# Opening a graph-network tile with three slots bank by bank, kept products between the banks

## The reference

```python
h = jnp.maximum(_layernorm(x), 0.0)
weight = jnp.einsum('rb,bio->rio', w_comp, bases)       # 32 relations from 8 bases
h_rel = jnp.einsum('ni,rio->rno', h, weight)
x = x + jax.ops.segment_sum(h_rel[etype, src] * norm, dst, num_segments=n) + h_bias
h = jnp.maximum(_layernorm(x), 0.0)
# second layer: every edge and every self loop, norm = dis[row] * dis[col], dis = rsqrt(degree)
x = x + jax.nn.relu(jax.ops.segment_sum(norm * (h @ W.T + b)[row], col, num_segments=n))
```

## Time and profile before

| | us |
|---|---|
| median of 3 runs | 644.56 |
| lowest, highest | 641.9, 646.03 |
| the profiled execution | 644.92 |
| its span, first to last instruction | 643.0 |
| PE busy in it | 514.1 (80%) |
| POOL busy in it | 342.6 (53%) |

### The profile page before, as it was taken

One profiled execution on the slowest core, in us unless ns is written; L12 is line 12 of the kernel. 1 busy time (PEld: TensorE's weight loads), 2 busy tenths in 40 slices (PEclk: granted clock), 3 DMA queues, 4 the chain that ended last, 5 costly groups with the idle time before them and its releaser, 6 DMA issues.

```text
span 643.0 us, 16581 instructions
## 1 busy us (share of the span) xinstructions
PE 514.1 (80%) x6328; PEld 328.7 (51%) x6328; DVE 320.2 (50%) x894; ACT 151.5 (24%) x272; POOL 342.6 (53%) x466
## 2 busy tenths in 40 slices
PE   2221626658989999989999999998997877889997
PEld 1111515536656666656666556665655555545443
DVE  8995038865465345665654654554643221454121
ACT  3436235432122011221220310302201000240121
POOL 3105707864665776675756747767677777400000
PEclk9555657679999999999999999999999987789999
DMA  9639985654676787785875858868768788523042
GB/s 283 231 125 338 390 299 139 190 144 128 192 224 179 223 264 202 207 260 157 248 225 165 267 155 231 265 194 263 240 195 266 238 239 237 155 55 111 1 97 66
DMA packets 43606, 130.01 MB, mean 202 GB/s; under 512 B 8911, under 2 KB 9536, under 8 KB 43462
## 3 DMA queue, kind: packets, MB, share of 16 engines
q0 software_dynamic: 27040, 99.60, 52.4%
q1 hardware_dynamic: 15004, 27.08, 13.0%
q10 hardware_dynamic: 1482, 2.18, 1.0%
HBM read 120.39 MB, written 11.00 MB: 204 GB/s over the span
## 4 chain that ended last, share of the span: by engine, by line
PE 53%; DMA 9%; DVE 7%; issue 5%; ACT 3%; POOL 2%; ACTq 0%; DVEq 0%
PE PS L1482 23%; PE PS L1462 17%; DMA gath<-rows_layer,srcs 9%; PE PS L1558 7%; PE PS L1502 4%; DVE room_b L1177 2%; POOL gath L672 2%; DVE zt L1177 1%; PE PS L1468 1%; PE PS L1356 1%; ACT room_b L780 1%; PE PS L1491 1%; ACT zt L780 1%; PE PS L1364 1%; DVE sel L1099 0%
## 5 line engine op out<-in xcount | busy, mean ns | idle before, releaser
L672 POOL DMA_INDIRECT gath<-rows_layer,srcs x335 | 334.4, 998 | 198.9 <-PE PS L1468 104.3
L1462 PE MATMUL PS<-sel,gath 128*128 128x48 f16 (+7 forms) x4020 | 305.4, 209 | 58.0 <-DMA gath<-rows_layer,srcs 38.4
L1462 PEld LDWEIGHTS PS<-sel,gath 128*128 128x128 f16 x4020 | 236.6, 104 | 172.0 <-issue 93.0
L1482 PE MATMUL PS<-room_b,zt 128*128 128x512 f16 x480 | 168.3, 392 | 7.3 <-DVE room_b L1213 6.9
L1482 PE MATMUL PS<-room_b 128*128 128x512 f16 (+1 forms) x480 | 151.6, 384 | 0.2 <-DVE room_b L1177 0.2
L1468 PE MATMUL PS<-oh_ad,gath 128*128 128x30 bf16 (+7 forms) x335 | 65.6, 196 | 0.0
L1093 DVE TENSOR_TENSOR masks<-iota_n,dloc 128x24 f32<-128x24 f32 (+12 forms) x92 | 17.6, 191 | 94.8 <-PE PS L1468 60.0
L1482 PEld LDWEIGHTS PS<-room_b 128*128 128x128 f16 (+1 forms) x480 | 47.9, 105 | 14.8 <-issue 1.8
L730 ACT CAST val<-val_f 128x64 f16<-128x64 f32 x42 | 11.1, 263 | 183.8 <-DVE val_f L1043 183.8
L1482 PEld LDWEIGHTS PS<-room_b,zt 128*128 128x128 f16 x480 | 45.2, 100 | 14.4 <-issue 8.4
L1099 DVE TENSOR_TENSOR sel<-masks,val 128x192 f32<-128x192 f32 (+12 forms) x92 | 38.6, 420 | 0.0
(11 more groups left out here) (202 smaller groups left out, 408.1 us busy)
## 6 DMA issues: line engine op xcount, KB each, us to landing
room_b<-in_L_gnn_bases_dram SPq DMA_DIRECT2D x8, 1024.0 KB, 8.8
gath<-rows_layer,srcs POOLq DMA_INDIRECT x335, 4.1
x_base<-in_x_dram SPq DMA_DIRECT2D x1, 2500.0 KB, 37.9
x_t<-x_base SPq DMA_DIRECT2D x19, 128.0 KB
u_t<-in_x_dram SPq DMA_DIRECT2D x9, 256.0 KB, 6.5
x_layer<-x_t SPq DMA_DIRECT2D x18, 128.0 KB, 3.8
u_t<-x_layer SPq DMA_DIRECT2D x18, 128.0 KB, 2.7
out_dram<-u_t SPq DMA_DIRECT2D x18, 128.0 KB
```

What stands on the lines that cost most here:

```text
L672: pool.indirect_dma_start(out=gath[:, s % UN, :], out_offset=None, in_=tab0_d[:, :], in_offset=bass.IndirectOffsetOnAxis(ap=srcs[:, s:s + ...
L1462: mm(there, gath[:, s % UN, D * t + P * f:D * t + P * (f + 1)], sel_parts[:, here, k, 0:NB * w, u], start=first and t == 0 and u == 1, sto ...
L1482: last = mm(PS[0:r, PBANK[q], :], zt[q % 2][:, t, f, b, 0:r], base_hl[:, b, u, f, :], start=(m == 0), stop=(m == NM - 1))
```

## The change

For every tile but the first in order (r = 0), the first OPEN = 3 slots are issued as one group. PE first waits for all three gathers, then goes bank by bank: three narrow matmuls of each of the three slots into bank 0, the same nine into bank 1, and so on, and the three count matmuls at the end. The 14 kept products are spread over the group: seven ahead of bank 0, then two ahead of banks 1, 2 and CB and one ahead of bank 3. The work of STEPS and the products that stood between the three slots come behind the group; these products are spread over the fourth slot. The loads of the column places for all three slots are made ahead of the group. The planner, POOL, DVE and ACT programs stay as they are.

```diff
-            def edges(s, at, wide):
-                r = TILE_AT[s]
-                n, w = BATCH_AT[s], WIN[r]
-                here, k = n % SRING, s - BATCHES[n][0]
-                pe.wait_ge(s_gathered[s % UN], 16 * (s // UN + 1))
-                if k == 0:
-                    pe.wait_ge(s_sel, n + 1)
+            def edges(group, wide):
+                s0 = group[0][0]
+                r = TILE_AT[s0]
+                w = WIN[r]
+                opens = s0 == S0[r]
+                for s, _ in group:
+                    pe.wait_ge(s_gathered[s % UN], 16 * (s // UN + 1))
+                    if s == BATCHES[BATCH_AT[s]][0]:
+                        pe.wait_ge(s_sel, BATCH_AT[s] + 1)
...
+                narrow = (3 * FT + 1) * len(group)
                 slack = [0] * narrow
...
+                for j in range(len(wide)):
+                    if not opens:
                         slack[1 + j * (narrow - 1) // len(wide)] += 1
+                    elif j < len(wide) // 2:
+                        slack[0] += 1
+                    else:
+                        slack[3 * len(group) * (1 + j % FT)] += 1
...
                 for f in range(FT):
+                    for s, at in group:
+                        here, k = BATCH_AT[s] % SRING, s - BATCHES[BATCH_AT[s]][0]
+                        there = zbank(f)[:, :, bass.ds(at, w)]
+                        for t, u in ((0, 1), (0, 0), (1, 1)):
+                            between()
+                            if s == S0[r] and r and (t, u) == (0, 1):
+                                pe.wait_ge(s_lo, FT * (r - 1) + f + 1)
+                            mm(there, gath[:, s % UN, D * t + P * f:D * t + P * (f + 1)],
+                               sel_parts[:, here, k, 0:NB * w, u], start=s == S0[r] and t == 0 and u == 1, stop=True,
+                               skip_group_check=True)
+                for s, at in group:
...
+                    between()
+                    if s == S0[r] and r:
+                        pe.wait_ge(s_ci, r)
+                    mm(there, oh_r[:, s % UN, :], oh_ad[:, here, k, 0:HA * w], start=s == S0[r], stop=True,
+                       skip_group_check=True).then_inc(s_used, 1)
...
             for s in range(VEND):
-                if s < SL:
-                    edges(s, window.pop(s), wide)
+                r = TILE_AT[s] if s < SL else 0
+                if s < SL and not (r and S0[r] < s < S0[r] + OPEN):
+                    n = OPEN if r and s == S0[r] else 1
+                    edges([(k, window.pop(k)) for k in range(s, s + n)], wide)
                     wide = []
```

More of the change, by code:

```diff
@@ L537, in gnn_kernel @@
         BEGUN = 5
+        OPEN = 3
+        assert min(SLOTS) >= OPEN and OPEN <= BQ < WPACK * (WLOAD - 1)
         @block.sync
@@ L1429, in slot_windows, with between @@
                     window[n] = begin.with_bounds(min_val=0, max_val=TN - WIN[TILE_AT[n]])
-            def edges(s, at, wide):
-                r = TILE_AT[s]
-                n, w = BATCH_AT[s], WIN[r]
-                here, k = n % SRING, s - BATCHES[n][0]
-                pe.wait_ge(s_gathered[s % UN], 16 * (s // UN + 1))
-                if k == 0:
-                    pe.wait_ge(s_sel, n + 1)
-                first = s == S0[r]
-                narrow = 3 * FT + 1
-                slack = [0] * narrow
[L1443 to L1447, removed]
-                        slack[1 + j * (narrow - 1) // len(wide)] += 1
-                def between(j):
-                    for m in wide[sum(slack[:j]):sum(slack[:j + 1])]:
+            def edges(group, wide):
[8 more added lines that the diff above has]
+                narrow = (3 * FT + 1) * len(group)
+                slack = [0] * narrow
+                for j in range(len(wide)):
+                    if not opens:
+                        slack[1 + j * (narrow - 1) // len(wide)] += 1
+                    elif j < len(wide) // 2:
+                        slack[0] += 1
+                    else:
+                        slack[3 * len(group) * (1 + j % FT)] += 1
+                done = [0, 0]
+                def between():
+                    for m in wide[done[1]:done[1] + slack[done[0]]]:
@@ L1452, in between @@
                         product(*m)
+                    done[1] += slack[done[0]]
+                    done[0] += 1
                 for f in range(FT):
[L1457 to L1469, removed]
+                    for s, at in group:
[8 more added lines that the diff above has]
+                               skip_group_check=True)
@@ new lines, in edges @@
+                for s, at in group:
+                    here, k = BATCH_AT[s] % SRING, s - BATCHES[BATCH_AT[s]][0]
+                    there = PS[:, CB, 0:HA * TN].rearrange("p (a n) -> p a n", n=TN)[:, :, bass.ds(at, w)]
+                    between()
[3 more added lines that the diff above has]
+                       skip_group_check=True).then_inc(s_used, 1)
@@ L1471, in product @@
+                assert done[1] == len(wide)
             def product(q, lo, hi):
@@ L1539, in _ @@
                         product(q, lo, hi)
-                if s + 1 < SL and s + 1 not in window:
-                    slot_windows(s + 1)
+                r = TILE_AT[min(s + 1, SL - 1)]
+                n = OPEN if r and s + 1 == S0[r] else 0 if r and S0[r] < s + 1 < S0[r] + OPEN else 1
+                for k in range(s + 1, min(s + 1 + n, SL)):
+                    if k not in window:
+                        slot_windows(k)
             def gcn(j, qs):
```

## The result

The changed kernel takes 670.77 us in the median of 4 runs (668.04 to 672.39); beside it on the same chip the kernel before took 645.29 (641.9 to 648.13). The ratio is 1.0384, 95% interval 1.0354 to 1.0414: slower by 25.5 us, where 17.4 were predicted, and 0.8 us above the upper end of the range, 670. The profiled execution took 671.64 us, its span is 669.8 against 643.0.

What follows compares the result with a forecast made beforehand. No engine was taken as full: waits tie PE and POOL together, POOL delivering a slot every 1.25 us at best. Terms -3.7 + 17.1 - 1.1 + 5.1 = +17.4 us on 644.56 gave 662.0 us, range 650 to 670.

Steps and rivals of the forecast that it cites:

- (d): At the head of the group, PE waits for three gathers at odd tiles 7 to 19: +17.1 us.
- (f): TensorE's clock falls to its lower level behind new waits of about 3 us: three falls, +5.1 us.
- (c): Behind the group's opening, moved narrow matmuls and steps and the first slot's later release cost about nothing.
- wait without the clock: Rival: (a), (d) and (e) alone, with no clock falls, +12.3 us, 656.9 us; chance 0.27.
- the mark that I had named against (c): Sign in the changed profile: (c) is wrong if POOL's waits for line 1468 grow in the even tiles.
- (a): One more product ahead of bank 0 shortens its wait by up to 0.22 us at 17 openings: -3.7 us.
- (b): Nine narrow matmuls per bank gain nothing with products; tiles 1 and 2 save about 1 us each, then lose it.
- (e): After the openings, PE arriving later finds some gathers landed: 1.1 us back, bounds 0 and 4.

Runs made afterwards that it cites:

- e5: The changed kernel, but narrow matmuls of slots two and three read the first slot's rows, their gathers awaited only before their count matmuls; 648.61 against 646.2 us, ratio 1.0044.
- e14_wt: The changed kernel with the four transposes of W after slots 43 to 46 instead of 38 to 41, outside tile 3's group; 664.91 against 647.16 us, ratio 1.0258.
- e12: The changed kernel with ten products issued again ahead of the waits at tiles 9, 11, 13, 15 and 17; 661.68 against 646.42 us, ratio 1.0224.
- e17_slack: The kernel before's slot order, no groups, with only the first slots' products spread as in the change; 645.08 against 645.28 us, ratio 0.9983.
- e17_six: The changed kernel with groups of three only at tiles 4, 5, 8, 10, 12 and 14, and late waits; 641.63 against 645.28 us, ratio 0.9936.
- e11_late_waits: The changed kernel with the waits for gathers two and three just ahead of their own first narrow matmul in bank 0; 651.78 against 647.28 us, ratio 1.0080.
- e16_two: The changed kernel with groups of two slots instead of three; 648.82 against 645.31 us, ratio 1.0057.

## Why the prediction was right or wrong, by its steps

**(d), the wait for three gathers: right, a little too small.** 20.6 us in 8 waits for 17.1 in 7. Reckoned tile by tile: 7 1.4 (predicted 2.7), 9 2.0 (2.1), 11 2.6 (1.2), 13 3.8 (3.0), 15 3.9 (2.9), 17 3.0 (2.3), 19 3.0 (2.9). Tile 16, where I had written that the third gather is there long before, waited 1.0. At tiles 13 and 15 a gather took 5.4 and 6.4 us from issue to PE's start, where I had taken 4.9 with 5.5 as the end: other gathers were issued right before and after it, and the DMA share was 0.85 to 0.89. Whether they slowed it no run shows. e5 shows that this wait and what hangs on it are 22.7 of the 25.5 us.

**(f), the clock: the right mechanism, a size that is right by luck.** I forecast three falls; it fell behind tiles 11, 13, 15 and 17, and in tile 3. The price can be read from the ledger: an opening grows by what its idle time grew, and by the fall. At tiles 7, 9 and 16, without a fall, growth less added idle time is 0.0 to -0.2; at 11, 13, 15 and 17 it is 1.3, 1.3, 1.5 and 1.3. One opening was seen both ways: tile 9 waited 1.97 us in the change, with no fall, and opened 1.3 us slower than before; in e14_wt it waited 1.92 us, the clock fell, and it opened 2.6 us slower. So a fall costs 1.3 to 1.5 us here, not 1.7, and four cost 5.4 us for the 5.1 predicted: one more fall, each a little cheaper. The fifth belongs to (c). The rival "wait without the clock" is out by these differences and by e12.

**(c), the moved steps: the step that failed.** I priced it at "about nothing" and wrote that types and look "only change places". I had not gone through the steps of each opening one by one. At tile 3 three steps that share one bank came to stand in a row: +2.3 us, by e14, the fall of the clock among them. At tiles 16 and 17 `types` came to stand right behind another step on that bank: 0.8 and 1.4 us of new waits, in all five traces of this kind with groups of three there, and at most 0.2 us in e17_slack and e17_six. That is 4.5 us where I had put nothing.

I had said too that the release of the first slot, late by 0.6 to 1.4 us, would cost nothing. The rest of the tiles 6, 8 and 18, which run at POOL's pace, got 1.7, 0.8 and 2.2 us longer. POOL's waits for PE, the mark that I had named against (c), are no witness: they grew by 17 us over those of the earlier trace rows, but between tiles 3 and 19 by only 2.3 us in the even tiles and by 13.7 in the odd ones, where PE itself waits. For tile 18 the group is the likely cause: the five runs with a group of three there show +0.7 to +2.2, e17_slack and e17_six, which have none, about 0. For tile 6 the same five show +1.0 to +1.7 and e17_six, which has no group there, +0.4; e17_slack has none either and shows +2.1, but its clock fell at 229.7 us in that tile, behind idle times of 0.4 and 1.4 us. No run took the late release away by itself, so this part stays open.

**(a), one more product ahead: the mechanism was wrong.** I took -3.7 us for 17 shorter waits. e17_slack has the extra product and no group: it shortens the waits and not the openings, and gained at most 2.5 us by its interval. In the change the waits for a bank fell by 12.4 - 6.9 = 5.5 us, and the openings without a late gather became 5.2 us shorter. So the gain is of the forecast's size by luck; it comes with the group.

**(b), nine narrow matmuls to a bank: half right.** Tiles 1 and 2 open 0.9 and 1.7 us faster and lose 2.0 and 1.7 in their rest, as forecast. That with products the order "gains nothing" was wrong: six openings got 3.3 us shorter in e17_six, and next to nothing (0.3 us) in e17_slack. Which part of the new order does it, the longer work per bank or the waits between slots that fall away, no run separates.

**(e), what comes back: -1.1 predicted, about 0.** The waits of narrow matmuls for gathers did not shrink, 38.2 for 38.4.

Together: (d) 20.6 for 17.1, (f) 5.4 for 5.1, (c) 2.3 + 2.2 + 3.6 (the rests of tiles 6 to 18, whose cause is open) for 0, (e) 0 for -1.1. For the -3.7 of (a) stand the 5.2 us of the openings that got shorter and 2.2 us of waits that the eight waiting ones no longer have. With 0.5 us left over in those eight, 1.4 us up to tile 3 and -1.6 behind slot 334 that is 27.0, for a span longer by 26.8. What the range lacked was (c), priced at nothing and with no bound above nothing.

## What to carry to other kernels

A wait put at the head of a group takes the latest of its members, and everything queued on the engine behind it pays, also the work that was put there to cover another wait: put each wait at the first instruction that needs it (+5.2 us in place of +25.5 here), and group only where the producer is ahead (4 us faster than before here). Read how far ahead it is at the very place, from the issue of the last member to the start of the group, not from an average. And when steps move into one another, list what each of them shares (a bank, a buffer), since neighbours that were harmless with work between them wait for each other without it.

## What the runs showed of the hardware

- An idle time of PE of 2.6 to 3.9 us in a stretch otherwise full of matmuls put the clock from 1.00 to 0.50 for about 3.4 us behind it, and the opening took 1.3 to 1.5 us longer than its idle time explains. After 1.0 and 1.4 us the clock stayed at 1.00 in the change; in e17_slack it fell behind 1.39 us with 0.41 us shortly before, and at tile 3 of the change behind two idle times of 1.56 us. The length of the one wait doesn't decide: 1.97 us in the change (0.82 us idle shortly before) and 2.06 in e11_late_waits left the clock at 1.00, 1.92 us in e14_wt (0.69 us idle shortly before) and 2.29 in e16_two brought it to 0.50. Matmuls put into the waits kept it at 1.00: with 11 us more work in them, five openings of e12_busy took 9.0 us less than in the change.
- A gather of 128 rows took 3.9 us in the median from issue to landing. The third gathers of tiles 13 and 15 took 5.4 and 6.4 us from issue to the start of PE that waited for them, in stretches with a DMA share of 0.85 to 0.89.
- The same program ran in 642 or in 744 us of span, in one series or the other, with some 100 idle times of PE ahead of the narrow matmuls that nothing in the profile explains. A change whose cost lies in late transfers can't be judged in the longer kind: groups of two read 1.0004 to 1.0032 there and 1.0057 in the other, late waits 1.0003 and 1.0009 against 1.0080.
